# Second sweep of a graph kernel: GpSimd waits before quads 1 to 3 of each chunk for score products of the chunk ahead of it

## What is computed

```python
h = relu(layernorm(x))
x = x + L0(h, src, dst)          # relu(relu(((1+eps)*h + segment_sum(h[src], dst)) @ W1 + b1) @ W2 + b2)
h = relu(layernorm(x))
x = x + L1(h, edge_index, edge_weight1, edge_attr_128)

# L1
hn   = layernorm(x) * gamma + beta
t    = gelu(concat([hn[src], edge_vector], 1) @ Wt + bt)
q    = hn[dst] @ Wq + bq
k    = t @ Wk + bk
attn = sum(k * q, -1) * edge_type / sqrt(D)
a    = exp(attn - max over the edges of dst) / (sum of those exps over dst + 1e-16)
out  = x + gelu(segment_sum(a * (t @ Wv + bv), dst))
```

## Time and profile before

| | |
|---|---|
| median of 3 runs, not profiled | 4087.96 us |
| the profiled execution, first to last instruction | 6013.6 us |
| TensorE (PE) busy | 3985.3 us, 66% |
| GpSimd (POOL) busy | 3043.9 us, 51% |
| VectorE (DVE) busy | 1961.7 us, 33% |
| ScalarE (ACT) busy | 1601.6 us, 27% |
| mean granted TensorE clock | 0.633 |
| moved by DMA | 446.29 MB, 74 GB/s over the span |

### The profile page before, as it was taken

One profiled execution on the slowest core, in us unless ns is written; L12 is line 12 of the kernel. 1 busy time (PEld: TensorE's weight loads), 2 busy tenths in 40 slices (PEclk: granted clock), 3 DMA queues, 4 the chain that ended last, 5 costly groups with the idle time before them and its releaser, 6 DMA issues.

```text
span 6013.6 us, 75137 instructions
## 1 busy us (share of the span) xinstructions
PE 3985.3 (66%) x19120; PEld 3071.2 (51%) x19121; DVE 1961.7 (33%) x6898; ACT 1601.6 (27%) x3223; POOL 3043.9 (51%) x3332
## 2 busy tenths in 40 slices
PE   1466666555555555577777777777777777777777
PEld 1344444444434444355555555556555565555655
DVE  4222222222222222233333333333333333333344
ACT  4222222222222222322222222222222222222223
POOL 4566666666666666344444444444444444444442
PEclk5555555555565555577766667766676666766677
DMA  4122222222222222222222222222222222222222
GB/s 128 53 68 66 65 67 66 65 67 67 66 65 68 66 65 67 62 81 77 81 77 77 82 76 80 78 78 81 75 81 77 76 82 76 81 77 77 82 77 65
DMA packets 390065, 446.29 MB, mean 74 GB/s; under 512 B 111768, under 2 KB 314734, under 8 KB 390000
## 3 DMA queue, kind: packets, MB, share of 16 engines
q1 hardware_dynamic: 276940, 233.83, 13.3%
q0 software_dynamic: 100096, 205.20, 13.1%
q10 hardware_dynamic: 12964, 6.53, 0.4%
HBM read 387.05 MB, written 58.21 MB: 74 GB/s over the span
## 4 chain that ended last, share of the span: by engine, by line
another core or an unknown queue 28%; PE 25%; ACT 3%; issue 2%; DVE 0%; DVEq 0%; ACTq 0%
PE attention_sum_ps L1210 10%; PE attention_t_ps L1153 4%; PE attention_pre_ps L1144 3%; PE attention_sc_q L1167 3%; PE attention_row_bank L1189 2%; PE attention_pre_ps L1140 2%; ACT attention_tT L1281 2%; ACT attention_t L1285 1%; PE attention_tot_ps L1219 1%; PE attention_tot_ps L1202 1%; PE attention_sum_ps L1201 0%; DVE attention_lines L1419 0%; ACT acc L1043 0%; PE attention_xm_bank L1175 0%
## 5 line engine op out<-in xcount | busy, mean ns | idle before, releaser
L514 POOL DMA_INDIRECT attention_t<-source_rows,attention_idx x1548 | 1471.4, 951 | 496.0 <-issue 496.0
L514 POOL DMA_INDIRECT gin_hs<-h_rows,gin_idx x1500 | 1455.8, 971 | 486.1 <-issue 486.1
L508 POOL TENSOR_TENSOR spare<-ones 1x1 f32<-1x1 f32 x195 | 36.0, 184 | 1892.9 <-PE attention_sum_ps L1210 1376.9
L1281 ACT ACTIVATE attention_tT<-attention_pre_ps 128x512 f32<-128x512 f32 x391 | 233.5, 597 | 1883.5 <-remote 1381.9
L1167 PE MATMUL attention_sc_q<-attention_qw,attention_tT 128*128 x3128 | 590.7, 329 | 187.7 <-issue 187.6
L1167 PEld LDWEIGHTS attention_sc_q<-attention_qw,attention_tT 128*128 128x128 f32 x3128 | 540.7, 247 | 215.6 <-issue 215.4
L698 PE MATMUL gin_sums<-gin_hot,gin_hs 128*128 128x40 f32 x3136 | 612.2, 383 | 0.0
L1210 PE MATMUL attention_sum_ps<-attention_e_hot,attention_t 128*128 128x96 f32 x3072 | 607.5, 389 | 0.0
L698 PEld LDWEIGHTS gin_sums<-gin_hot,gin_hs 128*128 128x128 f32 x3136 | 598.1, 297 | 18.2 <-issue 12.6
L1210 PEld LDWEIGHTS attention_sum_ps<-attention_e_hot,attention_t 128*128 128x128 f32 x3072 | 591.8, 301 | 21.4 <-issue 20.9
L706 PE MATMUL gin_uy_bank<-acc,gin_w_W 128*128 x196 | 118.6, 708 | 727.2 <-DVE acc L926 727.1
(11 more groups left out here) (215 smaller groups left out, 5319.1 us busy)
## 6 DMA issues: line engine op xcount, KB each, us to landing
attention_evT<-in_edge_attr_cols SPq DMA_DIRECT2D x196, 512.0 KB
attention_t<-source_rows,attention_idx POOLq DMA_INDIRECT x1548
gin_hs<-h_rows,gin_idx POOLq DMA_INDIRECT x1500
attention_qw<-qk_cols SPq DMA_DIRECT2D x98, 160.0 KB, 3.2
attention_cw<-qk_bias_cols SPq DMA_DIRECT2D x98, 132.0 KB, 3.9
attention_fade<-fades SPq DMA_DIRECT2D x98, 132.0 KB, 3.8
gin_x<-in_x SPq DMA_DIRECT2D x98, 128.0 KB
residual_rows<-gin_r SPq DMA_DIRECT2D x98, 128.0 KB
```

The lines of the kernel that those rows point to most:

```text
L514: gp.indirect_dma_start(out=out[:, k, :], out_offset=None, in_=rows[:, :], compute_op=op, in_offset=bass.IndirectOffsetOnAxis(ap=idx[:, k: ...
L1281: act.activation(tT[q % 2][:, :], pre_ps[:, :], ACT.Gelu).then_inc(s["tT_sb"], 1)
```

## The change

GpSimd gets three more stops per chunk in the second sweep. In front of quad q (1, 2, 3) of chunk c it waits until TensorE has done the score products of quad q-1 of chunk c-1, and then makes another `hold`. The counting of `held` changes with it from one to four per chunk. For chunk 0 only the `hold` is added (the wait's value would be negative, and `wait` leaves it out). The last chunk has three quads and so two more stops. That makes 293 more `hold` instructions, and no transfer more or less.

```diff
@@ -1120,8 +1120,11 @@
                                 gp.wait_ge(w["tables"], 7)
                             wait(gp, idx_in[f.j], 16 * (f.h + f.j))
                             wait(gp, s["t_used"], PARTS * (f.c - 3))
-                            hold(gp, g, held, f.c)
+                            hold(gp, g, held, QUADS * f.c)
                             for q in range(QUADS - 1 if f.last else QUADS):
+                                if q > 0:
+                                    wait(gp, s["sc_q"], QUADS * (f.c - 1) + q)
+                                    hold(gp, g, held, QUADS * f.c + q)
                                 gather_chunk(gp, g["idx0"] if f.at == 0 else idx[f.j], arow, t[f.k], gathered[f.k][q],
                                              cols=range(4 * q, 4 * q + 4))
```

## The result

The changed kernel takes 4115.57 us (median of 4 runs, 4110.78 to 4124.43), against 4087.18 us (4085.53 to 4090.1) of the kernel before on the same chip: 28.4 us more, a ratio of 1.007 with a 95% interval of 1.0058 to 1.0083. The forecast was 4111 us.

A forecast was written before the change was run, and what follows sets the result against it. GpSimd's issue of gathers was taken to set the pace; 293 holds at 0.08 us add 23 us, waits and register operations nothing: 4088 + 23 = 4111 us. Own range 4096 to 4130 us; 8 in 10, 4068 to 4180.

The forecast's parts named there:

- What bounds the kernel: Both sweeps: GpSimd's issue of gathers sets the pace outside the profile, 3937 us of the 4088.
- the late completions: TensorE's completions, seen up to ten microseconds late while gathers are issued; claimed to exist under the profiler only.
- Term 1: GpSimd, second sweep: 293 more holds at 0.08 us each, +23 us.
- Term 2: GpSimd's new waits on score products: met in time, slacks 6.6, 8.6 and 9.0 us, so 0 us.
- Term 3: Register operations for the waits' values on GpSimd's sequencer: from 0 to 105 us, taken as computed ahead.
- TensorE's step: TensorE's time per full chunk: 19.5 to 20.4 us, within half a microsecond of GpSimd's 20.12.
- no change: Rival: TensorE's step is the longer one and the added holds disappear in GpSimd's idling, 4088 us; chance 0.22.
- Faster: Rival: TensorE's delays are partly real outside the profile and the stops let completions through, 4062 us; chance 0.13.
- Slower by more: Rival: waits asked for before met, or registers not computed ahead, 0.36 us per stop, 4193 us; chance 0.15.
- What would show it: Profile after: 488 holds, next gather 1.29 us after a met hold, third stop waiting, span perhaps hundreds of microseconds shorter.
- A gather's landing: Quad 3's landing after its issue, used for the waits' slacks: 3.2 us, from the row of a 160 KB load.

The follow-up runs named there:

- before_again: The kernel before, unchanged, profiled once more: 4077.64 us, profiled span 4076.0 us.
- holds_seven: The changed kernel without its score-product waits and with seven extra holds per chunk instead of three (684 more than before): 4148.65 us, ratio 1.0162.
- holds_only: The changed kernel without its waits on the score products, all 293 holds kept: 4108.66 us, ratio 1.006.
- one_later: The changed kernel with every second-sweep stop asking for one score product more: 4108.37 us, ratio 1.0066.
- after_again: The changed kernel run once more, no edit: 4111.96 us, ratio 1.0074 against the kernel before.
- experiment 5: The changed kernel with all stops of a chunk asking for four score products of the chunk ahead (4427.66 us), or for three (4274.85 us).
- three_of_four: The changed kernel with all stops of a chunk asking for three of the four score products of the chunk ahead: 4274.85 us, ratio 1.0474.

## Why the prediction was right, and where not

**What bounds the kernel: right, shown.** The forecast set the old profile's span aside and took single durations: 195.5 x 20.12 us of issue in a time of 4088. The undisturbed profile has 20.2 us per chunk, and leaving out one gather takes off nearly its 1.25 us. Of the first sweep only the trace speaks, since no experiment touched it: in `before_again` its holds wait 36 us in all, 29.6 of them for the normalised rows. That the late completions do not occur in ordinary runs was argued then; the profile taken again, an execution of the ordinary 4077.64 us, has none.

**Term 1, the holds: right in kind, somewhat too small.** 0.08 us was predicted. The first group of runs gives 0.097 us (28.4 / 293; 0.081 to 0.116 by the interval) and `holds_seven` 0.096 us (684 holds; 0.088 to 0.106), while `holds_only` and `one_later`, with 293 holds each, give 0.087 and 0.085. The traces say 0.08 to 0.09: the two pitches around a hold give 1.30 + 1.29 - 2 x 1.25 = 0.09 us, and the second sweep is 26.8 us longer, 26.8 / 293 = 0.091, or 23.3 us by the profile of `after_again` (from its first gather to its last 1999.9 us), 0.079. So a hold costs about 0.09 us; no interval reaches down to 0, but whether it is 0.08 or 0.10 isn't settled. I had taken 0.08 from one chunk, as a difference of two numbers of some 20 us, in which an error of 0.01 us is nothing to either of them; a value over many chunks wasn't to be had undisturbed from the old profile's second sweep.

**Term 2, the waits: right.** Predicted slacks were 6.6, 8.6 and 9.0 us. Over 75 chunks of the changed kernel's trace the products end -4.1, 0.9 and 5.5 us after the chunk's hold (medians), and GpSimd asks at 5.1, 10.2 and 15.3: slacks of 9.2, 9.3 and 9.8 us, at the least 7.2, 7.2 and 7.7. (The least of the whole sweep is 4.5 us, in its first chunks.) The forecast was too careful since it read TensorE's places from a step that it held to be 20.4 us long, and counted 3.2 us from the end of a quad's issue to its landing, where TensorE starts on quad 3 after 1.7. Without the waits the time is the same (experiment 2), and with waits one product later also (4).

**Term 3, the register operations: right at 0.** Their upper bound was 105 us. `holds_only` against the changed kernel leaves 3.3 us for the waits and their register work together, no more than the spread of the runs. `holds_only` keeps the register work for `held` itself; for that the rows at 3013.45 speak, a stop inside the loop, whose hold starts 0.02 us after the gather before it ended, like the one without register operations in the earlier trace rows.

**TensorE's step: wrong, without harm to the sum.** "Within half a microsecond of each other" was the forecast's main uncertainty: 19.5 to 20.4 us against 20.12. It is 18.5 us. The error is in how the last chunk was read: of the 20.4 us, 1.6 are the sum products, taken at 5.44 us from a stretch with a granted clock of 0.69. At full clock they take 3.81, and the step before in the same trace had them so:

```profile
5955.76 3.81 PE L1210 MATMUL attention_sum_ps<-attention_e_hot,attention_t 128*128 128x96 f32 x32
```

With it the same sum gives 18.8 us, not the "nearer 19.5" of the prediction. The rival "no change" stood on this number; with 1.7 us between the engines it had no ground.

**The rivals.** Faster: refuted, nothing is late in a profiled execution of the ordinary length, and the change brought no gain. Slower by more: its mechanism exists (experiment 5) but begins only where the stop asks for the third product, not the first; there it costs 165 us.

**What would show it: half wrong.** 488 holds and a pitch of 1.29 to 1.30 us over a met hold came as said. That the third stop would wait in the profile did not. The profiled span did get shorter by 1904 us, as I had held possible, but not for my reason, that stops let the late completions through: the unchanged kernel, profiled again, has lost them as well. I had taken the disturbance for something that a profile of this kernel always has. The Trainium skill's rule ("NOTIFIC — the notification-queue block", Overflow, back-pressure from the trace writer) would put such delays down to the profiler; the runs fit it as far as no unprofiled run has them, but none shows the block or why the same kernel has them once and once not.

**A gather's landing: too long for the quad it was used on.** The prediction took 3.2 us. Beside it stood an estimate of 2.2 us after the issue, worked out from the Trainium skill's "DMA: Bandwidth & Descriptors" (Anatomy of one DMA); the traces have 2.6 us from the start of the issue in the first sweep of the changed kernel, so the estimate is 0.4 us short:

```profile
gin_hs<-h_rows,gin_idx POOLq DMA_INDIRECT x1500, 2.6
```

The issue itself takes 0.95 of these 2.6 us, which fits the 1.7 us from the end of quad 3's issue to TensorE's start on it.

## What to carry to other kernels

On the engine that sets the pace even a met wait has a price: count the instructions that carry it, here some 0.09 us each, 25 to 29 us for 293. Whether a wait binds is read over many iterations, not in one, and when it does bind, add up the whole ring (issue, landing with what else is then being loaded, the consumer's work up to the signal, clock included): one ring of 21.3 to 23.3 us beside engines of 20.4 and 18.5 us cost more than all the met waits together. And where a profiled span is far from the unprofiled time, profile the same kernel again before explaining any difference between two profiles.

## What was not expected of the hardware

- The same kernel, profiled twice, had spans of 6013.6 and 4076.0 us; in the first, ScalarE stood up to 17.7 us ahead of a GELU for completions of TensorE that were seen late, in the second none came late. The cause stays open.
- After 3.14 us of standing still TensorE came back at half clock (0.50 granted), and the slower products fed the very wait that had made it stand still. After 2.52 us in the trace of `three_of_four` it came back at full clock (1.00 in the next 2.4 us), after 2.74 and 2.81 us its clock fell within the next products (0.56 and 0.53 in the 2.9 and 2.3 us from the second product on):

```profile
3023.62 0.65 PE L1143 MATMUL attention_pre_ps<-ident,attention_t 128*128 128x128 f32 x4 [2.52 <-DMA attention_t<-source_rows,attention_idx]
3024.11 1.02 PE L1147 MATMUL attention_pre_ps<-attention_evT,attention_w_edge 128*128 128x512 f32 x2
...
3045.21 0.66 PE L1143 MATMUL attention_pre_ps<-ident,attention_t 128*128 128x128 f32 x4 [2.81 <-DMA attention_t<-source_rows,attention_idx]
3045.71 1.77 PE L1147 MATMUL attention_pre_ps<-attention_evT,attention_w_edge 128*128 128x512 f32 x2
```

  The length of the pause alone does not decide it. In the changed kernel a pause of 2.21 us was followed by a granted clock of 0.54 over the next 2.0 us (first row), and in the kernel before, profiled again, one of 2.93 us by 1.00 over the next 3.7 us (second row):

```profile
3898.80 0.98 PE L1143 MATMUL attention_pre_ps<-ident,attention_t 128*128 128x128 f32 x4 [2.21 <-DMA attention_t<-source_rows,attention_idx]
3765.32 0.65 PE L1140 MATMUL attention_pre_ps<-ident,attention_t 128*128 128x128 f32 x4 [2.93 <-DMA attention_t<-source_rows,attention_idx]
```

- A one-element multiply of 0.18 us between two gathers costs only some 0.09 us, since the gap to the gather behind it shrinks from 0.30 to 0.15 us.
